# A summed buffer for three slots, one fold a part, and selectors made in place

## What is computed

```python
x = x + _L0_conv_ref(_gn(x), ...)   # 3x3 convolution from 6x6 Winograd weights
x = x + _L1_conv_ref(_gn(x), ...)   # deformable convolution, 9 taps, bilinear samples
x = x + _L2_conv_ref(_gn(x), ...)   # four binary-weight 3x3 convolutions, quantised activations
x = x + _L3_conv_ref(_gn(x), ...)   # 3x3 convolution + edge term, channel attention
```

```python
corners = [(y0, x0, (y0 + 1 - py) * (x0 + 1 - px)), (y0, x0 + 1, (y0 + 1 - py) * (px - x0)),
           (y0 + 1, x0, (py - y0) * (x0 + 1 - px)), (y0 + 1, x0 + 1, (py - y0) * (px - x0))]
...
y = jnp.einsum('bgikhw,goik->bgohw', s, wg)
```

## Time and profile before

| | |
|---|---|
| median of 3 runs (lowest, highest) | 4327.13 us (4326.23, 4340.27) |
| profiled execution, span | 4328.9 us |
| TensorE busy | 4115.4 us, 95% |
| VectorE busy | 3191.3 us, 74% |
| ScalarE busy | 1827.2 us, 42% |
| GpSimd busy | 3159.8 us, 73% |
| granted TensorE clock, mean | 0.983 |

### The profile page before, as it was taken

One profiled execution on the slowest core, in us unless ns is written; L12 is line 12 of the kernel. 1 busy time (PEld: TensorE's weight loads), 2 busy tenths in 40 slices (PEclk: granted clock), 3 DMA queues, 4 the chain that ended last, 5 costly groups with the idle time before them and its releaser, 6 DMA issues.

```text
span 4328.9 us, 61705 instructions
## 1 busy us (share of the span) xinstructions
PE 4115.4 (95%) x21925; PEld 1924.0 (44%) x21925; DVE 3191.3 (74%) x6460; ACT 1827.2 (42%) x2008; POOL 3159.8 (73%) x3094
## 2 busy tenths in 40 slices
PE   2899999999999999999999999999999999999993
PEld 2444444444444444444444444444444444444441
DVE  4757787777877777787777877877787777877663
ACT  1344444444444434444444444444444444444431
POOL 1777777777777777777777777777777777777750
PEclk8899999999999999999999999999999999999996
DMA  4677787878878788887877878787887878878762
GB/s 111 216 234 245 238 263 220 265 227 248 256 235 263 227 250 258 245 256 229 261 233 246 270 233 261 223 251 249 245 258 232 258 234 253 260 237 258 240 194 64
DMA packets 480231, 1022.57 MB, mean 236 GB/s; under 512 B 262164, under 2 KB 298356, under 8 KB 475636
## 3 DMA queue, kind: packets, MB, share of 16 engines
q1 hardware_dynamic: 283252, 460.40, 34.7%
q10 hardware_dynamic: 98400, 356.97, 25.4%
q0 software_dynamic: 98304, 201.52, 16.5%
HBM read 862.19 MB, written 73.20 MB: 216 GB/s over the span
## 4 chain that ended last, share of the span: by engine, by line
PE 72%; DVE 13%; POOL 5%; issue 4%; DMA 3%; SPq 1%; ACTq 1%; ACT 1%; POOLq 0%; DVEq 0%
PE ps_r L1506 52%; PE ps_c L1492 5%; POOL ring L599 5%; PE ps_y L1521 4%; PE ps_a L1445 3%; DVE col_hat L1198 2%; PE ps_c L1535 2%; PE ps_a L1492 2%; DMA taps_c<-plane_act 1%; PE ps_y L1542 1%; DVE ps_w L1219 1%; DVE ring L1225 1%; PE ps_a L1483 1%; DVE ring L1221 1%; ACTq L793 1%
## 5 line engine op out<-in xcount | busy, mean ns | idle before, releaser
L599 POOL DMA_INDIRECT ring<-patch_table,idx_part x3072 | 3151.6, 1026 | 1031.6 <-issue 1019.6
L1506 PE MATMUL ps_r<-select,image 128*128 128x512 f32 x6912 | 3160.9, 602 | 21.1 <-DVE col_hat L1198 15.3
L1506 PEld LDWEIGHTS ps_r<-select,image 128*128 128x128 f32 x6912 | 1253.6, 190 | 1424.3 <-issue 1368.9
L1198 DVE TENSOR_TENSOR col_hat<-ps_r,col_hat 128x512 f32<-128x512 f32 x1152 | 790.6, 686 | 919.1 <-PE ps_r L1506 917.8
L649 ACT ACTIVATE select<-row_in,minus_row 128x1536 f32<-128x1536 f32 x384 | 604.8, 1575 | 1042.7 <-PE ps_r L1506 556.9
L651 ACT ACTIVATE select<-select,one_col 128x1536 f32<-128x1536 f32 x384 | 605.3, 1576 | 12.5
L668 ACT COPY samples<-ps_c 128x512 f32<-128x512 f32 x256 | 148.9, 582 | 655.8 <-PE ps_c L1535 655.8
L1219 DVE TENSOR_TENSOR ps_w<-ring,ps_w 128x384 f32<-128x384 f32 x512 | 284.8, 556 | 19.8 <-DMA ring<-patch_table,idx_part 15.2
L1225 DVE TENSOR_TENSOR ring<-ring,ps_w 128x384 f32<-128x384 f32 x512 | 280.3, 547 | 4.4
L1221 DVE TENSOR_TENSOR ring<-ring,ps_w 128x384 f32<-128x384 f32 x512 | 280.2, 547 | 0.0
L1521 PEld LDWEIGHTS ps_y<-col_hat,w_dense 128*32 128x32 f32 x6144 | 143.5, 109 | 297.5 <-issue 245.9
(11 more groups left out here) (233 smaller groups left out, 2588.9 us busy)
## 6 DMA issues: line engine op xcount, KB each, us to landing
col_hat<-coord_table SPq DMA_DIRECT2D x384, 768.0 KB
row_in<-coord_table ACTq DMA_DIRECT2D x384, 768.0 KB
ring<-patch_table,idx_part POOLq DMA_INDIRECT x3072
taps_c<-plane_act SPq DMA_DIRECT2D x135, 268.1 KB
coord_table<-wino ACTq DMA_DIRECT2D x64, 216.0 KB
taps_c<-xn_c ACTq DMA_DIRECT2D x96, 130.0 KB
taps_c<-xn_c SPq DMA_DIRECT2D x96, 130.0 KB
plane_act<-act_c SPq DMA_DIRECT2D x180, 65.0 KB
```

What stands on the lines that cost most here:

```text
L599: nc.gpsimd.indirect_dma_start(out=ring[j][:, h % 2, k, :], out_offset=None, in_=table, in_offset=bass.IndirectOffsetOnAxis(ap=idx_part[:, ...
L1198: v.tensor_tensor(hat_t, ps_r[:, (s + t) % 2], hat_t, ALU.mult).then_inc(tile_weighed, 1)
L1506: ins = mm(ps_r[:, (s + t) % 2], image[:, m, t], select[s % 2][:, m], start=(m == 0), stop=(m == PAIRS - 1))
```

## The change

The three tiles of a slot are now summed in every slot, into a buffer of their own, `dense_sum`, which has a place for each of the three slots of a part. The product of the first tile stays in `col_hat`; those of the second and third are written back to their PSUM bank, and an add takes them from there. `tile_weighed` rises behind the add for these two, so a bank is released after two instructions in place of one. TensorE folds the three sums of a part together, once, behind the second row tile of the next part, in front of the gathered blocks' folds, which came behind the first row tile before. The second tile of a part's first slot waits for that fold (`dense_folded`). The column loads wait for the weighing and not for the fold.

The selectors are made in place: the load writes `select`, both activations run in it, and there are three such buffers; `row_in` is gone. The load of slot s+2 now stands behind the selectors of slot s+1 and waits for the row tiles of slot s-1. On VectorE and TensorE the first steps of stage C move by one tile.

```diff
-        row_in = [sb(f"row_in{b}", [P, PAIRS, HALF]) for b in range(2)]
-        select = [sb(f"select{b}", [P, PAIRS, HALF]) for b in range(2)]
+        select = [sb(f"select{b}", [P, PAIRS, HALF]) for b in range(3)]
         col_hat = [sb(f"col_hat{b}", [P, WT, HALF]) for b in range(3)]
+        dense_sum = sb("dense_sum", [P, DT, HALF])
...
                 if not known_zero(n) or s >= 3:
-                    sp.wait_ge(dense_folded, n * SLOTS + s - 2)
+                    sp.wait_ge(tile_weighed, (n * SLOTS + s - 2) * WT)
...
-                if not known_zero(n) or s >= 2:
-                    act.wait_ge(row_in_read, n * SLOTS + s - 1)
+                if not known_zero(n) or s >= 3:
+                    act.wait_ge(rows_made, (n * SLOTS + s - 2) * WT)
...
             def make_select(n, s):
-                u = n * SLOTS + s
-                act.wait_ge(row_in_in[s % 2], (n * (SLOTS // 2) + s // 2 + 1) * 16)
-                if not known_zero(n) or s >= 2:
-                    act.wait_ge(rows_made, (u - 1) * WT)
-                sel = select[s % 2][:]
-                nc.scalar.activation(sel, row_in[s % 2][:], ACT.Abs, bias=minus_row[:]).then_inc(row_in_read, 1)
-                act.wait_ge(row_in_read, u + 1)
+                act.wait_ge(rows_in[s % 3], (n * (SLOTS // 3) + s // 3 + 1) * 16)
+                sel = select[s % 3][:]
+                nc.scalar.activation(sel, sel, ACT.Abs, bias=minus_row[:]).then_inc(distance_made, 1)
+                act.wait_ge(distance_made, n * SLOTS + s + 1)
                 nc.scalar.activation(sel, sel, ACT.Relu, bias=one_col[:], scale=-1.0).then_inc(select_made, 1)
...
                 dve.wait_ge(rows_made, tile + 1)
-                hat_t = col_hat[s % 3][:, t]
-                v.tensor_tensor(hat_t, ps_r[:, (s + t) % 2], hat_t, ALU.mult).then_inc(tile_weighed, 1)
...
+                hat_t, rows_t = col_hat[s % 3][:, t], ps_r[:, (s + t) % 2]
+                if t == 0:
+                    v.tensor_tensor(hat_t, rows_t, hat_t, ALU.mult).then_inc(tile_weighed, 1)
+                    return
+                g, e = divmod(s, DT)
+                chain.step(v.tensor_tensor(rows_t, rows_t, hat_t, ALU.mult))
+                dve.wait_ge(tile_weighed, tile)
+                if t == 1 and e == 0 and (not known_zero(n) or g > 0):
+                    dve.wait_ge(dense_folded, n * PARTS + g)
+                first_term = col_hat[s % 3][:, 0] if t == 1 else dense_sum[:, e]
+                v.tensor_tensor(dense_sum[:, e], first_term, rows_t, ALU.add).then_inc(tile_weighed, 1)
...
-            def fold_dense(n, s):
-
-                g, e = divmod(s, DT)
-                if e == 0 and (not known_zero(n) or g > 0):
+            def fold_dense(n, g):
+
+                if not known_zero(n) or g > 0:
                     pe.wait_ge(conv_saved, n * PARTS + g)
-                for t in range(1 if s in SUMMED else WT):
-                    if s in SUMMED:
-                        pe.wait_ge(tiles_summed, n * len(SUMMED) + SUMMED.index(s) + 1)
-                    else:
-                        pe.wait_ge(tile_weighed, (n * SLOTS + s) * WT + t + 1)
+                for e in range(DT):
+                    pe.wait_ge(tile_weighed, (n * SLOTS + g * DT + e + 1) * WT)
                     for j in range(JB):
                         ins = mm(ps_y[j * C:(j + 1) * C, :],
                                  w_dense[:, DT - 1 - e].rearrange("p g o -> p (g o)"),
-                                 col_hat[s % 3][:, t, j * P:(j + 1) * P], start=(e == 0 and t == 0), stop=False)
+                                 dense_sum[:, e, j * P:(j + 1) * P], start=(e == 0), stop=False)
...
-                    if q == 0:
-                        fold_before(n, s)
+                    if q == 1 and e == 0:
+                        fold_before(n, g)
```

More of the change, by code:

```diff
@@ L41 @@
 DSEL = DT * Q
-SUMMED = (4, 5, 6, 7, 8, 11, 14, 19, 20, 21, 22, 23)
 ITEMS = DT * PARTS
@@ L295, in build @@
         coords_out = sem("coords_out")
-        row_in_in = [sem(f"row_in_in{b}") for b in range(2)]
+        rows_in = [sem(f"rows_in{b}") for b in range(3)]
         col_hat_in = [sem(f"col_hat_in{b}") for b in range(3)]
@@ L1617, in slot, with fold_before @@
                         first(n + 2, s, q)
[L1619 to L1621 removed]
+            def fold_before(n, g):
+                n, g = (n, g - 1) if g > 0 else (n - 1, PARTS - 1)
                 if not live(n):
                     return
[L1624 to L1628 removed]
+                fold_dense(n, g)
+                for k in range(CHUNKS):
+                    fold(n, g, k)
             schedule(pe, Chain(pe, None), slot, prepare_rest)
```

41 lines of the change are left out of this document (11 added, 30 removed).

## The result

The changed kernel takes 4465.86 us (median of 4 runs, 4457.52 to 4470.61) against 4332.97 us (4326.23 to 4340.27) on the same chip: a ratio of 1.0304, with a 95% interval of 1.0285 to 1.0322. I had forecast 4360 with a range up to 4402. The sign was right, and the loss is four times what I forecast (133 us against 33).

What follows compares the result with a forecast made beforehand. TensorE was taken to set the pace, except in slots 7 to 10, where VectorE does. Fourteen images at +3.1 us (+43), last -6.5, first -3: +34, 4363, stated as 4360 us; 8 in 10 range 4300 to 4402.

Steps and rivals of the forecast that it cites:

- rival 2: Row loads behind ScalarE's selectors, only one under way: 3 us an image slower if ScalarE falls behind, 4410; chance 0.08.
- What I cost at nothing: Wait for dense_folded, column loads, save_conv one row tile later, stage C's first steps moved: all costed at zero.
- (c): Slots 15 to 17: adds of 4.4 us against 4.0 idle; slot 19 starts about 1.0 us later.
- Folds removed, adds put on: TensorE saves 7.5 us of folds an image; VectorE gets 24 more adds, 17.5 us an image.
- (a): Slots 1 to 3: VectorE comes 3.8 us later, TensorE has 1.9 in hand; slot 5 starts 1.9 us later.
- (b): Slots 7 to 10: four adds, 2.9 us, against 0.2 us of idle; slot 11 starts 2.7 us later.
- The remaining slots: Outside the three stretches: folds count in full, -3.3 us, later bank releases some 0.8; leaves -2.5 us an image.
- The sums together: Whole kernel: the forecast's total of all terms over the sixteen images, +34 us.
- Rival 1: TensorE's saving arrives, limited by the gathers, which may get shorter: 4261 to 4324, about 4300 us; chance 0.25.
- The forecast's own range: Whole kernel: the forecast, chance 0.55, with 4340 to 4385 us from +1.5 to +4.5 an image over fourteen.
- the 9.5 and the 1.8: Savings of last (-6.5) and first image (-3); profiled execution 1.8 us above the median of the runs.

Runs made afterwards that it cites:

- e4: Changed kernel with the row load put back ahead of ScalarE's early steps and selectors, three buffers kept: 4439.00 us, ratio 1.0244.
- e16: Kernel before with selectors made in place in three buffers, row load still ahead of them: 4407.93 us, ratio 1.0171.
- e17: Changed kernel with row loads issued by SyncE and x loads moved from slot 10 to slot 15: 4384.51 us, ratio 1.0124.
- e13: Changed kernel with four calls (eight throwaway matmuls) added ahead of TensorE's wait for the taps in slot 11: 4422.15 us, ratio 1.0207.
- e1: Changed kernel without the adds in the 12 slots not summed before; doesn't compute the reference: 4351.29 us, ratio 1.0043.
- e9: Changed kernel with nine calls of throwaway matmuls, longer than the wait, ahead of the taps wait in slot 11: 4454.47 us, ratio 1.0289.
- e8: Changed kernel with SyncE's x loads moved from slot 10 to slot 13: 4398.10 us, ratio 1.0147.

## Why the prediction was wrong

The step that failed is in rival 2: "the load that was issued two slots ahead has up to 18 us, so I expect ScalarE to stay ahead". On it rest the forecast's nothing for the selectors' part (under "What I cost at nothing" the row load isn't even named) and the 0.08. I asked of the moved load only whether the selectors would have it in time. ScalarE's wait did grow (144.0 to 479.4 us), but with it taken down to 95.3 (e4) only 27 us came back, and in e16 it never grew while 78 us were lost. What I didn't ask is where in the slot a 768 KB transfer now lies and what else is in flight. The taps load of slot 11 has no term in the prediction: it had 10.4 us from issue to use, and nothing in hand for another large transfer. Against e17, which has the same sums, that step is 3.7 us an image in slot 11 and 1.4 in slot 12, 81 us in all; 1.9 of it is the lower clock behind the wait (e13: 0.5 in slot 11, 1.4 in slot 12). The second and smaller failure is (c), below.

Point by point:

- **Folds removed, adds put on.** Right in size: 687 ns an add (0.69), product into PSUM 694 against 686, VectorE busy +254 (265 forecast). TensorE's fold saving doesn't show as 120 us of busy time, since the lower clock stretched other matmuls; in e17, where it falls less, PE is busy 4009 us, 106 less than before. As time it arrives only in part, 4.0 us an image outside slots 11 and 12 (e1).
- **(a) slots 1 to 3.** +1.9 by the means, 1.6 in the eighth image; forecast 1.9. Right.
- **(b) slots 7 to 10.** +1.7; forecast 2.7. VectorE's busy time in the stretch rose by 1.6 (37.62 less 36.02). Only three of the four adds that I counted stand ahead of the moments (2.1 us), and one 0.55 us operation on `ring` fell out of the stretch.
- **(c) slots 15 to 18.** +3.5; forecast 1.0. The mechanism is as I wrote it, the size is off by the clock. TensorE's timeline of the changed kernel, from the first tile of slot 18:

```profile
2182.73 2.74 PE L1495 MATMUL ps_r<-select,image 128*128 128x512 f32 x6
2187.42 0.38 PE L1408 MATMUL ps_c<-mv_c,same_channel 128*128 128x1 f32 x2 [1.95 <-DVE mv_c L931]
2187.67 4.52 PE L1495 MATMUL ps_r<-select,image 128*128 128x512 f32 x6
2192.11 0.86 PE L1506 MATMUL ps_y<-dense_sum,w_dense 128*32 128x128 f32 x24
```

  The moments come 35.2 us after slot 15's start, where TensorE asked for them at 34.7 before, and the 1.2 us of folds now stand behind: 1.7 against 1.0. The next row tile then takes 4.52 us instead of 2.84, at the lower clock: 1.7 more that I had no term for. In e9, where the clock falls in slot 18 of one image only (13 here), the stretch is +2.0.
- **The remaining slots.** Forecast -2.5 with slots 11 and 12 in it. The other nine gave -1.9; slots 11 and 12 gave +4.9 where some -0.4 was due.
- **The sums together.** Forecast +34, by e17 +55: the sign was right, and the size is off by (c), +3.1 there against 1.0, less what (b) came out smaller (+1.6 against 2.7). That the two errors have opposite signs is luck.
- **The other things at nothing.** The wait for `dense_folded` cost 10.5 us of VectorE's time in all. That held. The move of stage C's first steps was not tried apart.
- **Rival 1.** Gathers did get shorter, 1026 to 1009 ns, and it bought nothing, because TensorE and VectorE had become later than they. **Rival 2** named the right load and a wrong mechanism, and at 3 us an image and a chance of 0.08 was too small in both. Half of its sign came, ScalarE waiting for row loads; the other half, TensorE waiting for `select`, did not (2.9 us in the run).
- **The forecast's own range.** +1.5 to +4.5 us an image, less the 9.5 and the 1.8, gives 4339 to 4381, not 4340 to 4385; it changes nothing here.

No version here beats the kernel before. The adds cost 7.8 us an image (267.76 less 259.93), the folds give back 4.0 of their 7.5 (e17 has 4.4 us more an image than the kernel before), and the best of the changed ones that compute the reference, e17, is 1.2% slower.

## What to carry to other kernels

When a change moves the issue of a large load, look for every transfer that is in flight at the new place and for its first user's slack: read the slack (here 10.4 us from issue to use) as a number, as you would an engine's. Fewer buffers move a load in time as surely as an edit of the order does, even if its own reader never waits for it. And price a new wait of TensorE at more than its length: here 3.2 us of waiting in slot 11, on average, were followed by a lower clock that cost another 1.9 us.

## What the runs showed of the hardware

- A taps load of 3 x 268 KB landed in under 10.4 us with column loads and x loads in flight, and took 14.5 us with a row load of 768 KB beside them as well; in that slot the DMA engines were busy 1.01 of the time at 283 GB/s. Without the x loads, but with the row load, TensorE no longer waited (e8: 0.88, 260 GB/s). Full DMA engines alone are not the sign: in e17, without the x loads, slot 11 of the eighth image has 1.01 as well, at 315 GB/s, and no wait. Why a row load beside the x loads delays the taps so much is not shown.

```profile
2065.86:2078.07 12.21, 12.21 (x54) 5.44 (x54) 8.17 (x19) 5.11 (x6) 9.18 (x10) 0.86 1.01 315
```

- After TensorE's wait for the taps of slot 11 (3.2 us on average, at most 4.6) the granted clock was 0.5 for the convolution or the next row tile or two in 14 of 15 images. With the wait filled by 2.7 us of throwaway matmuls it fell behind it in none, and the kernel was 44 us faster.
- The falls are not settled by the wait just ahead of them alone. In slot 18 the changed kernel waits 1.95 us and the clock falls; e9 has a wait of 1.96 at the same place in the same image, without a fall, and only slot 11 differs. Over the run slot 18 has 13 falls in the changed kernel, 7 in e13, 1 in e9, and 10 in e17, which has hardly a wait in slot 11; and where the line of e17 above shows a clock of 0.86, it fell at the start of slot 11, behind a wait of 1.79 us for the moments that every image has there, and in one other image only. What links them stays open. Slot 18 of that image as a window, in the changed kernel and in e9:

```profile
2182.74:2196.17 13.43, 11.48 (x65) 5.13 (x63) 9.01 (x22) 4.34 (x7) 4.41 (x5) 0.87 1.02 287
```

```profile
2169.76:2181.51 11.75, 9.79 (x63) 4.73 (x62) 9.00 (x21) 4.37 (x5) 3.55 (x4) 1.00 1.01 282
```
